# Row-group scores and a three-deep pipeline in linear attention; normalised probabilities, weighed two tiles at a time, in softmax attention

## The chip, the cores and the metric
The kernel runs on one core of a Trainium2 chip. The core's engines run side by side, each with its own queue, and wait for each other by semaphores: PE (TensorE, matmuls and transposes into PSUM), DVE (VectorE), ACT (ScalarE), POOL (GpSimd, SBUF only) and SP, which issues DMAs. The metric is the time of one execution on the device in microseconds; smaller is better.

## The reference
The input x is 2 sequences of 1024 tokens of 256 features. Two halves follow each other, all in fp32:

```
x = x + layernorm(linear_attention(layernorm(x)))          # 16 heads of 16, chunks
x = x + layernorm(h + moe(rmsnorm(h))),  h = t + attention(rmsnorm(t)),  t = layernorm(x)
```

The linear attention makes q = (x Wq f1 + b1)(x Wq f2 + b2), the same for k, and o = q (sum of earlier k'v) + masked(q k') v, then an rms norm over each head's 16 features and a projection. The kernel takes chunks of 128 tokens, which gives the same sums. The softmax attention is causal, with 32 query heads of 64 features and 8 key/value heads: scores, softmax, weighing of the values, projection. Then every token goes to its best 2 of 8 experts.

## The kernel before
Each engine has its own program; the order of work is written out by hand. A semaphore counts steps, and a later step waits for a count.

**Linear attention.** A step `s` of 8 handles 128 tokens of both batch entries (a pair of tiles). `pair_step(s, front, back)` exists on each engine: its front makes xn (normalised x), its transpose xnT, four feature products (q1, q2, k1, k2), qT and kT, v, the scores and kv of tiles `s`; its back makes output, rms norm, projection, residual and the norms of tiles `s-1`, and writes them turned into `rT_all`. So each step runs the front of one pair and the back of the one before; steps 1 to 7 are a hardware loop. Scores (L1113 to L1121): `qx` holds q eight times, each time with all but one head's 16 rows set to zero by `headmask` (POOL for k=0, L457; ACT for k=1, L582); a matmul over all 128 rows then gives four heads' scores for 512 columns. DVE masks each of four halves of scores (L774). DVE also adds to the running state (L791) and adds the residual (L822). `power` (L443) on POOL is the inverse root, three times per back.

**Softmax attention.** There are 16 sequences (8 key/value heads times 2 batch entries), each of 8 query tiles `ct` of 128 tokens; tile number `t` runs over 128. A tile has 4 heads and ct+1 blocks of 128 keys, so its scores are 128 x 128(ct+1) for each head: 128 columns for the first tile, 1024 for the last. Step `t` of the main loop does, on PE in this order:

- `score(t,0)`, the values (`values`, L1313) of tile t-2, `score(t,1)`, a third of the blocks of tile t-1 turned (`turn_part`, L1301), `score(t,2)`, the second third, `project_out` of tile t-2 (L1322), `score(t,3)`, the last third, and `project` of an item of the next half sequence (L1253, or L1243 for v).

DVE takes the maximum of each head's scores and copies them to SBUF (`maximum`, L884), ACT makes the exponentials in place with their sums (`exponent`, L640). Scores have four PSUM banks for ct<4 and two double banks above. The turned blocks go through three banks in rotation (`bank_of`, order in `TURNS`), which the items share, and are copied to SBUF by ACT and DVE in turn (L648, L892; `evacuate_part`). The division by the row's sum comes last: DVE takes the reciprocals (L905), POOL spreads them over 64 columns (L500), PE turns those too (L1298, one more block per tile, `m == t % TB + 1`), and DVE multiplies the weighed values by them (L909) into `oT`. `acc` gets the projection added by DVE (L922).

The change touches these two parts and nothing behind them but semaphore counts.

Of the kernel before, what the change touches and what calls it, by code (L numbers as in the profile page):

```python
# [10 lines left out]
ALU = mybir.AluOpType  # L11
# [26 lines left out]
NCONST = 27  # L38
# [23 lines left out]
def blocks_before(t):  # L62

    n, ct = divmod(t, TB)
    return n * (PAIRS + TB) + ct * (ct + 1) // 2 + ct
# [9 lines left out]
TURNS = FIRST_ITEMS + [x for t in range(TILES + 1)  # L75
                       for x in ([(t - 1, m) for p in range(3) for m in third(t - 1, p)] if t else []) + ([item_of(t)] if t < TILES and item_of(t) else [])]
# [8 lines left out]
def build(nc, a, out):  # L85
    ctx = ExitStack()
    with ctx:
# [23 lines left out]

        def x_part(x, part):

            return x[:].rearrange("p (b t) -> p b t", b=BATCH)[:, :, 1:TB] if part else x[:].rearrange("p (b t) -> p b t", b=BATCH)[:, :, 0:1]
# [21 lines left out]
        headmask = sb("headmask", [P, HB])  # L136
        experts = sb("experts", [P, E])
# [32 lines left out]
        qx = part(at, n, "p (k b h c) -> p k b h c", k=KB, b=BATCH, h=HB)  # L170
        sm = part(at + n, n, "p (k b h c) -> p k b h c", k=KB, b=BATCH, h=HB)
# [29 lines left out]
        onT = pair_tile(6)  # L201
        st6 = sb("st6", [P, BATCH, 6])
        mv = sb("mv", [P, BATCH, 2])
        ve = sb("ve", [P, BATCH])
        rstd = sb("rstd", [P, BATCH])
# [19 lines left out]
        rbc = [part(2 * G * SEQ + 2 * TB * G * P + i * 2 * P, 2 * P, "p (j c) -> p j c", j=2) for i in range(2)]  # L225
        spread = [part(2 * G * SEQ + 2 * TB * G * P + (2 + i) * 2 * P, 2 * P, "p (j c) -> p j c", j=2) for i in range(2)]
# [3 lines left out]
        def turned_to(t, m):  # L230

            src = bank_of((t, m))
            if m == t % TB + 1:
                return rbc[t % 2], src[:, 0:2 * P].rearrange("p (j c) -> p j c", j=2)
            return pT[t % 2][m], src[:]

        def evacuated(j):

            return S("pT_odd" if j % 2 else "pT_even"), j // 2 + 1
        oT = sb("oT", [P, 2, P])  # L240
# [86 lines left out]
        def _(sp):  # L327
# [36 lines left out]
            sp.wait_ge(S("acc_done"), BATCH * NKV * TB - TB)  # L364
            sp.dma_start(h_v[:, 0:TB], acc[:, 0:TB]).then_inc(S("h_stored"), 16)
            sp.wait_ge(S("acc_done"), BATCH * NKV * TB)
# [29 lines left out]
        def _(gp):  # L396
# [39 lines left out]
            nc.gpsimd.memset(state[:], 0.0).then_inc(S("constants_ready"), 1)  # L436
            gp.wait_ge(S("constants_ready"), NCONST - 1)
            nc.gpsimd.tensor_scalar(bd[:], headmask[:].rearrange("p (h o) -> p h o", o=1).to_broadcast([P, HB, DK]), 1.0 / DK, None, ALU.mult).then_inc(S("constants_ready"), 1)
# [12 lines left out]
            def pair_step(s, front, back):  # L451
                if front:
                    gp.wait_ge(S("qT_ready"), s + 1)
                    if front and back:
                        gp.wait_ge(S("scores1"), 4 * s)
                    for b in range(BATCH):
                        nc.gpsimd.tensor_tensor(qx[:, 0, b], qT[:, 0, b:b + 1, :].to_broadcast([P, HB, P]),  # L457
                                                headmask[:].rearrange("p (h o) -> p h o", o=1).to_broadcast([P, HB, P]),
                                                ALU.mult).then_inc(S("qx0_ready"), 1)
                if back:  # L460
                    for name in ("ao", "x1", "y"):
                        power(s - 1, BATCH, rstd[:], ve[:], "ve_" + name, "rstd_" + name)

            pair_step(0, True, False)
            x_power(1)
            with gp.Fori(1, TB) as s:
                pair_step(s, True, True)
            pair_step(TB, False, True)

# [19 lines left out]
            doubled = 1  # L489
            for t in range(TILES + 1):  # L490
                item = item_of(t - 1) if t else None
                if item and item[1] == 0:
                    if t > 1:
                        gp.wait_ge(S("rinv_spread"), t - 1)
                    double(item[0], item[2])
                    doubled += 1
                if t:
                    gp.wait_ge(S("k_doubled"), doubled)
                    gp.wait_ge(S("rinv_ready"), t)
                    nc.gpsimd.tensor_copy(spread[(t - 1) % 2].rearrange("p x (u d) -> p x u d", u=2),  # L500
                                          rinv[:, (t - 1) % 2].rearrange("p (u x o) -> p x u o", x=2, o=1).to_broadcast([P, 2, 2, DH])).then_inc(S("rinv_spread"), 1)
# [31 lines left out]
        def _(act):  # L533
# [18 lines left out]
            def pair_step(s, front, back):  # L552
                if front:
                    act.wait_ge(S("xnT_psum"), s + 1)
                    if back:
                        act.wait_ge(S("v_psum"), s)
                    nc.scalar.copy(whole(xnT[:]), bank[3][:]).then_inc(S("xnT_ready"), 1)
                if back:
                    act.wait_ge(S("o_psum"), s)
                    if front:  # L560
                        act.wait_ge(S("oms_psum"), s - 1)
                    nc.scalar.activation(whole(osq), bank[2][:], ACT.Square).then_inc(S("osq_ready"), 1)
                if front:
                    act.wait_ge(S("q1_psum"), s + 1)
                    if back:
                        act.wait_ge(S("qT_ready"), s)
                    nc.scalar.activation(whole(q1s), bank[0][:], ACT.Identity, bias=fbias_q[:, 0:1], scale=DK ** -0.5).then_inc(S("q1_ready"), 1)
                if back:
                    act.wait_ge(S("oms_psum"), s)
                    if front:  # L570
                        act.wait_ge(S("orstd_ready"), s - 1)
                    nc.scalar.activation(oms[:], bank[3][:], ACT.Sqrt, bias=eps[:, 0:1]).then_inc(S("oms_ready"), 1)
                if front:
                    act.wait_ge(S("k1_psum"), s + 1)
                    if back:
                        act.wait_ge(S("kT_ready"), s)
                    nc.scalar.activation(whole(k1s), bank[0][:], ACT.Identity, bias=fbias[:, 2:3]).then_inc(S("k1_ready"), 1)
                    act.wait_ge(S("qT_ready"), s + 1)
                    if back:
                        act.wait_ge(S("scores1"), 4 * s)  # L580
                    for h in range(HB):
                        ins = nc.scalar.activation(qx[:, 1, :, h], qT[:, 1], ACT.Copy, scale=headmask[:, h:h + 1])  # L582
                    ins.then_inc(S("qx1_ready"), 1)
                    act.wait_ge(S("v_psum"), s + 1)
                    if back:
                        act.wait_ge(S("kv_psum"), s)
                    for b in range(BATCH):
# [4 lines left out]
                if back:  # L592
                    tile = x_pairs(acc, s - 1)
                    act.wait_ge(S("y_ready"), s)
                    if front:
                        act.wait_ge(S("yss_ready"), s - 1)
# [3 lines left out]
                    wait_alone(act, S("rstd_y"), s)  # L600
                    if front:
                        act.wait_ge(S("rT_psum"), s - 1)
                    for b in range(BATCH):
                        ins = nc.scalar.activation(rn[:, b], tile[:, b], ACT.Copy, scale=rstd[:, b:b + 1])
                    ins.then_inc(S("r_ready"), 1)
                    act.wait_ge(S("rT_psum"), s)
                    for k in range(KB):
# [826 lines left out]
```

## Time and profile before

| what | value |
|---|---|
| median of 3 runs | 1934.72 us (1933.41 to 1934.87) |
| the profiled execution's own time | 1933.22 us |
| its span, first to last instruction | 1931.3 us |
| busy share: PE, DVE, ACT, POOL | 94%, 55%, 48%, 14% |
| chain that ended last: PE, DVE, ACT | 86%, 7%, 2% |
| mean granted TensorE clock | 0.976 |

The span is what the trace covers; 1.9 us of the execution lie around it. The chain that ended last is followed back from the last instruction to what released it each time; PE's share in it says on whose work the end hung. PE's busy time counts an instruction until its results have landed, so that back-to-back instructions overlap, and a busy PE is not one at its peak; its true pace shows in the distance between starts.

### The profile page before, as it was taken

The numbers are of one execution on the slowest core, as the hardware profiler recorded it, in microseconds if no ns is written. First come the engines' busy times: TensorE is split into PE (matmuls) and PEld (weight loads), VectorE is DVE, ScalarE is ACT, GpSimd is POOL, SyncE is SP. The second block draws the span as 40 slices with busy tenths as digits, with TensorE's granted clock in tenths as the row PEclk, the third lists the DMA queues.
The fourth block names the chain that finished last, engine by engine and source line by source line (L and its number), as shares of the span: only waits on it lengthen the run. The fifth ranks groups of instructions, "written<-read, shape, count | busy, mean of one in ns | idle before, by whom it ended". The sixth has DMA issues, their size and how long they took to land.

```text
span 1931.3 us, 32217 instructions
## 1 busy us (share of the span) xinstructions
PE 1813.6 (94%) x12286; PEld 1428.7 (74%) x12286; DVE 1055.0 (55%) x2465; ACT 924.1 (48%) x2049; POOL 261.1 (14%) x355
## 2 busy tenths in 40 slices
PE   6999689999999999999999999999985999999994
PEld 5666457777777777777777777777765999999993
DVE  3666556766776766767767667667655111111112
ACT  3343255655656656656656656656651222222223
POOL 2222110000000000000000000000001222222222
PEclk9999889999999999999999999999986999999997
DMA  2000010000000000000000000000017134213443
GB/s 83 0 0 0 0 44 1 9 1 1 9 1 1 9 1 1 10 1 1 9 1 1 9 1 1 1 1 1 23 34 245 22 92 128 48 26 87 119 125 95
DMA packets 46042, 60.02 MB, mean 31 GB/s; under 512 B 8944, under 2 KB 39536, under 8 KB 45936
## 3 DMA queue, kind: packets, MB, share of 16 engines
q1 hardware_dynamic: 36336, 46.16, 7.2%
q0 software_dynamic: 7536, 10.36, 3.2%
q10 hardware_dynamic: 2064, 2.10, 0.3%
q8 instruction: 66, 1.08, 0.2%
q14 instruction: 40, 0.33, 0.1%
HBM read 138.43 MB, written 11.40 MB: 78 GB/s over the span
## 4 chain that ended last, share of the span: by engine, by line
PE 86%; DVE 7%; ACT 2%; issue 2%; POOL 1%; DMA 1%; SPq 0%; DVEq 0%; POOLq 0%; ACTq 0%
PE wide L1401 15%; PE bank L1313 13%; PE bank L1301 12%; PE bank L1253 9%; PE wide L1285 8%; PE bank L1410 7%; PE wide L1286 7%; PE bank L1322 6%; PE wide L1120 2%; PE bank L1109 2%; PE bank L1298 1%; ACT qhl L634 1%; PE bank L1177 1%; DVE arena L802 1%; PE bank L1243 1%
## 5 line engine op out<-in xcount | busy, mean ns | idle before, releaser
L884 DVE CUSTOM_DVE_ANT_0 arena<-wide,arena 128x896 f32<-128x896 f32 (+7 forms) x512 | 383.8, 755 | 223.2 <-PE wide L1286 219.3
L640 ACT ACTIVATE arena<-arena,nmax 128x896 f32<-128x896 f32 (+7 forms) x512 | 397.0, 776 | 177.3 <-DVE nmax L884 174.2
L1285 PE MATMUL wide<-khi,qhl 128*128 128x512 f32 (+3 forms) x768 | 346.3, 452 | 1.7 <-DVE qhl L877 1.7
L1301 PE MATMUL bank<-ident,arena 128*128 128x128 f32 x2304 | 308.5, 274 | 0.0
L648 ACT COPY arena<-bank 128x512 f32<-128x512 f32 (+1 forms) x352 | 191.7, 545 | 214.0 <-PE bank L1301 206.3
L1401 PEld LDWEIGHTS wide<-wo,arena 128*128 128x128 f32 x2496 | 287.0, 193 | 3.2 <-issue 1.3
L1401 PE MATMUL wide<-wo,arena 128*128 128x128 f32 x2496 | 287.3, 277 | 0.9 <-ACT wo L693 0.9
L1313 PE MATMUL bank<-arena,vt 128*64 128x256 f32 x2304 | 277.0, 385 | 0.0
L1301 PEld LDWEIGHTS bank<-ident,arena 128*128 128x128 f32 x2304 | 262.3, 141 | 16.6 <-issue 0.4
L1286 PE MATMUL wide<-klo,qhl 128*128 128x512 f32 (+3 forms) x768 | 256.0, 347 | 0.0
L1050 DVE TENSOR_TENSOR wo<-wide,wo 128x512 f32<-128x512 f32 x78 | 53.9, 692 | 368.1 <-PE wide L1401 368.1
L892 DVE COPY arena<-bank 128x512 f32<-128x512 f32 (+1 forms) x352 | 222.9, 639 | 9.2 <-PE bank L1301 8.4
L1313 PEld LDWEIGHTS bank<-arena,vt 128*64 128x64 f32 x2304 | 154.2, 137 | 90.8 <-issue 19.9
L1285 PEld LDWEIGHTS wide<-khi,qhl 128*128 128x128 f32 x768 | 145.3, 189 | 89.3 <-issue 65.6
L1286 PEld LDWEIGHTS wide<-klo,qhl 128*128 128x128 f32 x768 | 146.2, 190 | 36.9 <-issue 22.5
L500 POOL COPY arena<-rinv 128x256 f32<-128x256 f32 x128 | 51.0, 398 | 784.4 <-DVE rinv L905 782.4
L1322 PE MATMUL bank<-wo,oT 128*128 128x256 f32 x512 | 135.1, 387 | 11.3 <-DVE oT L909 11.3
L1410 PE MATMUL bank<-arena,wo 128*128 128x256 f32 x624 | 141.2, 380 | 0.0
L703 ACT ACTIVATE wo<-wide 128x512 f32<-128x512 f32 x78 | 46.6, 597 | 170.3 <-PE wide L1401 170.3
L1410 PEld LDWEIGHTS bank<-arena,wo 128*128 128x128 f32 x624 | 115.8, 191 | 13.9
L1253 PE MATMUL bank<-rT_all,wq_g 128*128 128x512 f32 x256 | 122.5, 602 | 0.3
L1322 PEld LDWEIGHTS bank<-wo,oT 128*128 128x128 f32 x512 | 87.3, 191 | 24.3 <-DVE oT L909 14.7
(221 smaller groups left out, 1749.8 us busy)
## 6 DMA issues: line engine op xcount, KB each, us to landing
arena<-in_L_ffn_w SPq DMA_DIRECT2D x117, 1024.0 KB
x_all<-in_L_attn_x ACTq DMA_DIRECT2D x1, 2048.0 KB, 9.9
wq_g<-in_L_ffn_wq SPq DMA_DIRECT2D x8, 256.0 KB, 3.5
wo<-in_L_ffn_wo SPq DMA_DIRECT2D x16, 128.0 KB, 3.0
hbuf<-acc SPq DMA_DIRECT2D x2, 1024.0 KB, 4.6
tbuf<-rT_all SPq DMA_DIRECT2D x4, 512.0 KB, 3.0
acc<-hbuf SPq DMA_DIRECT2D x4, 512.0 KB, 5.5
out<-x_all SPq DMA_DIRECT2D x8, 256.0 KB, 2.1
```

Of the source, the lines that this page charges most:

```text
L640: nc.scalar.activation(probs[t % 2][:, h, 0:w], probs[t % 2][:, h, 0:w], ACT.Exp, bias=nmax[:, t % 2, h:h + 1], scale=-1.0, accum_out=rsum ...
L648: nc.scalar.copy(*turned_to(t, m)).then_inc(S("pT_even"), 1)
L884: nc.vector.tensor_tensor_reduce(out=probs[t % 2][:, h, 0:w], in0=score_bank(t, h)[:, 0:w], in1=causal[:, SEQ - w:SEQ], scale=-1.0, scalar ...
L892: nc.vector.tensor_copy(*turned_to(t, m)).then_inc(S("pT_odd"), 1)
L1253: ins = mm(to, w, rT_all[:, k, at:at + HALF], start=(k == 0), stop=(k == KB - 1))
L1285: mm(dst, q, khi[:, lo:lo + cols], start=True, stop=False)
L1286: ins = mm(dst, q, klo[:, lo:lo + cols], start=False, stop=True)
L1301: ins = nc.tensor.transpose(to[:, h * P:(h + 1) * P], probs[t % 2][:, h, m * P:(m + 1) * P], ident[:])
L1313: ins = mm(bank[2][u * DH:(u + 1) * DH, 0:2 * P], vt[:, n % 2, m], pT[t % 2][m][:, u * 2 * P:(u + 1) * 2 * P], start=(m == 0), stop=(m == ct))
L1322: ins = mm(bank[2][:, 2 * P:2 * P + D], oT[:, j], wo2[:, t // (BATCH * TB), j], start=(j == 0), stop=(j == 1))
L1401: ins = mm(wide[:, at + half, f * P:(f + 1) * P], w[:, k, (half * 4 + f) * P:(half * 4 + f + 1) * P], sT[u][:, k], start=(k == 0), stop=(k ...
L1410: ins = mm(bank[u][:, 0:D], gated[:, f], w2_e[u][:, f], start=(f == 0), stop=(f == FB - 1))
```

## The change
In linear attention the scores use four groups of 32 rows. `qx` holds q only twice (`rowmask`, heads even or odd within a group's 32 rows), and each matmul takes 32 rows and 256 columns into its own bank. The pipeline gets a third stage (output in step s+1, norms in s+2, turning in s+3), the loop is written out, the state and the residual are added on POOL, ACT normalises x (`normal_x`) and copies the projection's output (`aos`) out of PSUM.

In softmax attention DVE multiplies the probabilities by the reciprocal (`normalise`) before PE turns them; the spread block is gone, ACT copies all turned blocks and `oT`. The values of tiles t-3 and t-2 are weighed in one run, in steps of even number, into one bank, their projections go into a bank of the rotation, and one addition takes both.

```diff
-NCONST = 27
+NCONST = 29
+ROWS = 4
+HR = HB // ROWS
 def third(t, p):
-    blocks = t % TB + 2
+    blocks = t % TB + 1
     return range(blocks * p // 3, blocks * (p + 1) // 3)
+def weighed_in(t):
+    return [x for x in (t - 3, t - 2) if 0 <= x < TILES] if t % 2 == 0 else []
+STEPS = TILES + 3
+def turns_of(t):
+    turning = 1 <= t <= TILES
+    blocks = [[(t - 1, m) for m in third(t - 1, p)] if turning else [] for p in range(3)]
+    out = [("O", t)] if weighed_in(t) else []
+    item = [item_of(t)] if t < TILES and item_of(t) else []
+    return blocks[0] + blocks[1] + out + blocks[2] + item
...
 # POOL, linear attention
+                if back:
+                    power(s - 2, BATCH, rstds["ao"], ves["ao"], "ve_ao", "rstd_ao")
+                    gp.wait_ge(S("aon_ready"), s - 1)
+                    xb = x_pairs(x_all, s - 2)
+                    nc.gpsimd.tensor_tensor(xb, xb, aon, ALU.add).then_inc(S("x1_ready"), 1)
+                if mid and s < TB:
+                    gp.wait_ge(S("o_psum"), s)
+                    gp.wait_ge(S("kvt_ready"), s)
+                    nc.gpsimd.tensor_tensor(state, state, kvt, ALU.add).then_inc(S("state_ready"), 1)
...
 # DVE, order of a linear attention step
+                mask(s-1, 2), mask(s-1, 3); variance(ao), aon; qT; variance(x1); two reciprocals; kT; onT; y; mask(s, 0), mask(s, 1); ve_y; kvt
...
 # ACT, softmax attention
             def evacuate_part(t, p):
                 for m in third(t, p):
                     j = blocks_before(t) + m
-                    if j % 2 == 0:
-                        act.wait_ge(S("pT_psum"), j + 1)
-                        nc.scalar.copy(*turned_to(t, m)).then_inc(S("pT_even"), 1)
+                    act.wait_ge(S("pT_psum"), j + 1)
+                    nc.scalar.copy(pT[t % 2][m], bank_of((t, m))).then_inc(S("pT_ready"), 1)
...
                 if scored:
                     exponent(t, 0)
+                if weighed_in(t):
+                    n = 2 * P * len(weighed_in(t))
+                    act.wait_ge(S("o2_psum"), t // 2)
+                    nc.scalar.copy(oT[:].rearrange("p x j c -> p (x j c)")[:, 0:n], bank[2][:, 0:n]).then_inc(S("oT_ready"), 1)
...
 # DVE, softmax attention
+            def normalise(t, h):
+                w = (t % TB + 1) * P
+                if h % 2 == 0:
+                    invert(t, h // 2)
+                    v.wait_ge(S("rinv_ready"), 2 * t + h // 2 + 1)
+                nc.vector.tensor_scalar(probs[t % 2][:, h, 0:w], probs[t % 2][:, h, 0:w], rinv[:, t % 2, h:h + 1], None, ALU.mult).then_inc(S("probs_ready"), 1)
...
                 if scored:
                     maximum(t, 0)
+                if turning:
+                    normalise(t - 1, 2)
+                    normalise(t - 1, 3)
                 if item:
                     low_part(item)
...
                 if scored:
                     maximum(t, 2)
+                    normalise(t, 0)
+                if weighed_in(t):
+                    (adds the projection of both tiles to acc)
                 if scored:
                     maximum(t, 3)
+                    normalise(t, 1)
...
 # PE, linear attention
+                def score(k):
+                    pe.wait_ge(S("qx0_ready" if k == 0 else "qx1_ready"), s + 1)
+                    if s or k:
+                        pe.wait_ge(S("sm_ready"), 4 * s + 2 * k)
+                    for b in range(BATCH):
+                        for j in range(ROWS):
+                            rows = slice(j * P // ROWS, (j + 1) * P // ROWS)
+                            ins = mm(wide[:, j, b * HR * P:(b + 1) * HR * P], kT[rows, k, b], qx[rows, k, b].rearrange("p h c -> p (h c)"), start=True, stop=True)
 # order: output(0), turn xn, turn rn, feature 0, output(1), feature 1, mean square, features 2 and 3, v, turn kT, score(0), ao, kv, score(1)
...
 # PE, softmax attention
                     if m == 0:
-                        pe.wait_ge(S("exp_done"), G * (t + 1))
+                        pe.wait_ge(S("probs_ready"), G * (t + 1))
...
-                if weighing:
-                    values(t - 2)
+                if weighed_in(t):
+                    values(t)
```

Lines that begin with ` #`, and those that name steps in words, stand for longer stretches of the diff.

## Rows read from the trace of the kernel before

**Rows 1.** The page, part 1: busy time, share of the span, instructions.
```profile
PE 1813.6 (94%) x12286; PEld 1428.7 (74%) x12286; DVE 1055.0 (55%) x2465; ACT 924.1 (48%) x2049; POOL 261.1 (14%) x355
```

**Rows 2.** Windows: length, busy per engine, PE clock, DMA share, GB/s.
```profile
40.50:220.50 180.00, 168.92 (x1275) 118.92 (x1274) 117.76 (x204) 70.72 (x166) 40.87 (x35) 1.00 0.00 0
220.50:245.80 25.30, 8.87 (x112) 6.07 (x111) 10.66 (x21) 4.81 (x13) 2.09 (x3) 0.69 0.00 1
254.70:1428.00 1173.30, 1156.95 (x7405) 853.48 (x7406) 815.05 (x1948) 713.74 (x1563) 88.69 (x190) 1.00 0.02 4
```

**Rows 3.** Timeline, linear attention: start, length, engine, line, operation [idle before it].
```profile
117.94 0.43 PE L1131 MATMUL bank<-wo,arena 128*32 128x128 f32 x8
...
121.57 2.00 PE L1109 MATMUL bank<-arena 128*128 128x256 f32 x8
...
125.18 1.75 DVE L795 RECIPROCAL arena<-arena 128x256 f32<-128x256 f32 x1 [2.78 <-ACT arena L572]
...
127.67 3.75 POOL L457 TENSOR_TENSOR arena<-wo,headmask 128x1024 f32<-128x1024 f32 x2 [12.08 <-DVE wo L799]
...
128.50 3.29 ACT L582 ACTIVATE arena<-wo,headmask 128x256 f32<-128x256 f32 x8
...
133.94 3.60 PE L1120 MATMUL wide<-arena,wo 128*128 128x512 f32 x8
...
137.36 1.23 DVE L774 TENSOR_TENSOR arena<-wide,tri 128x1024 f32<-128x1024 f32 x1
...
138.50 0.72 DVE L831 TENSOR_SCALAR acc<-x_all,mv,rstd  x2
...
138.64 1.98 PE L1120 MATMUL wide<-arena,wo 128*128 128x512 f32 x4 [1.10 <-DVE arena L774]
139.14 1.22 DVE L774 TENSOR_TENSOR arena<-wide,tri 128x1024 f32<-128x1024 f32 x1
...
143.60 0.43 PE L1131 MATMUL bank<-wo,arena 128*32 128x128 f32 x8
```

**Rows 4.** Timeline: score(t,1) of the first tile of two successive sequences.
```profile
690.53 0.33 PE L1285 MATMUL wide<-khi,qhl 128*128 128x128 f32 x1
...
763.98 0.33 PE L1285 MATMUL wide<-khi,qhl 128*128 128x128 f32 x1
```

**Rows 5.** Timeline around a run of weighing and the maximum behind it.
```profile
1190.51 0.40 PE L1286 MATMUL wide<-klo,qhl 128*128 128x512 f32 x1
...
1190.84 2.81 PE L1313 MATMUL bank<-arena,vt 128*64 128x256 f32 x24
...
1193.91 0.40 PE L1286 MATMUL wide<-klo,qhl 128*128 128x512 f32 x1
...
1194.38 0.40 PE L1286 MATMUL wide<-klo,qhl 128*128 128x512 f32 x1
...
1194.82 1.23 DVE L884 CUSTOM_DVE_ANT_0 arena<-wide,arena 128x1024 f32<-128x1024 f32 x1 [0.55 <-PE wide L1286]
...
1195.97 0.08 DVE L884 DVE_READ_ACCUMULATOR2_ANT nmax<- 128x1 f32 x1
```

**Rows 6.** Timeline, end of the linear attention.
```profile
245.80 3.78 PE L1253 MATMUL bank<-rT_all,wkv_g 128*128 128x512 f32 x4 [0.93 <-ACT rT_all L608]
```

**Rows 7.** Groups by shape, softmax attention: busy us, mean ns | idle before, releaser.
```profile
L892 DVE COPY arena<-bank 128x512 f32<-128x512 f32 x288 | 196.5, 687 | 8.5 <-PE bank L1301 8.4
L640 ACT ACTIVATE arena<-arena,nmax 128x1024 f32<-128x1024 f32 x64 | 73.7, 1151 | 15.7 <-DVE nmax L884 15.7
...
L1298 PE MATMUL bank<-ident,arena 128*128 128x128 f32 x256 | 48.9, 273 | 1.4 <-POOL arena L500 1.4
```

**Rows 8.** Groups by shape, linear attention's loop: the same columns.
```profile
L819 DVE TENSOR_SCALAR arena<-bank,mv,rstd 128x256 f32<-128x256 f32 x14 | 7.0, 539 | 5.7 <-POOL rstd L443 5.7
...
L831 DVE TENSOR_SCALAR acc<-x_all,mv,rstd x14 | 5.1, 406 | 0.0
```

**Rows 9.** Groups by shape, softmax attention: the reciprocal.
```profile
L905 DVE RECIPROCAL rinv<-rsum 128x4 f32<-128x4 f32 x128 | 22.0, 172 | 3.5 <-ACT arena L640 0.8
```

More of the change, by code:

```diff
@@ L488, in _ @@
             double(0, 0)
[L489 to L501, printed above, removed]
+            for n in range(NSEQ):
+                for half in range(2):
+                    if n or half:
+                        double(n, half)
             gp.wait_ge(S("k_doubled"), 2 * NSEQ)
@@ L616, in _ @@
             act.wait_ge(S("ln_loaded"), 16 * (2 * KB + 1))
-            pair_step(0, True, False)
-            with act.Fori(1, TB) as s:
-                pair_step(s, True, True)
-            pair_step(TB, False, True)
+            normal_x(0)
+            for s in range(TB + 3):
+                pair_step(s)
             def evacuate(item):
@@ L653, in _ @@
                 evacuate(item)
-            for t in range(TILES + 2):
+            for t in range(STEPS):
                 scored, turning = t < TILES, 1 <= t <= TILES
@@ L1170, in pair_step @@
                     feature(bank[1], 3, "k2_psum")
-                if back:
+                    if mid:
+                        pe.wait_ge(S("oms_ready"), s)
+                    for b in range(BATCH):
+                        for k in range(KB):
+                            ins = mm(bank[3][:, b * D:(b + 1) * D], xnT[:, k, b], wvT[:, k], start=(k == 0), stop=(k == KB - 1))
+                    ins.then_inc(S("v_psum"), 1)
+                    pe.wait_ge(S("kT_ready"), s + 1)
+                    turn(bank[1], lambda k, b: kT[:, k, b], "ktok_psum")
+                    score(0)
+                if mid:
                     pe.wait_ge(S("onT_ready"), s)
@@ L1200, in pair_step @@
                     ins.then_inc(S("kv_psum"), 1)
[L1201 to L1211 removed]
+                    score(1)
+            for s in range(TB + 3):
+                pair_step(s, s < TB, 1 <= s <= TB, s >= 3)
             pe.wait_ge(S("rT_ready"), TB)
@@ L1326, in _ @@
                 project(item)
-            for t in range(TILES + 2):
-                scored, turning, weighing = t < TILES, 1 <= t <= TILES, t >= 2
+            for t in range(STEPS):
+                scored, turning = t < TILES, 1 <= t <= TILES
                 if scored:
                     score(t, 0)
-                if weighing:
-                    values(t - 2)
+                if weighed_in(t):
+                    values(t)
                 if scored:
@@ L1340, in _ @@
                     turn_part(t - 1, 1)
[L1341 to L1342 removed]
+                if weighed_in(t):
+                    project_out(t)
                 if scored:
```

419 lines of the change are left out of this document (193 added, 226 removed).

## The prediction
> **What bounds the kernel now.** I read the page's busy shares first: PE is busy 94% of the span, no other engine over 55% [rows 1]. A busy PE says little here, so the windows come next, one per stage, to see where the kernel spends its time: the linear attention's loop 180 us, its tail 25 us with PE busy 8.9 us, the softmax attention 1173 us [rows 2]. The router and experts behind them are not touched. Then the timeline, for start-to-start times, which a group's mean duration does not give. One loop step of the linear attention takes 143.60 - 117.94 = 25.66 us. One of the 16 sequences of the softmax attention takes 763.98 - 690.53 = 73.45 us [rows 3, 4].
>
> What PE must do in them. Eight feature instructions of 256 columns take 2.00 us, the last of them some 0.38 in flight: 0.213 each, 1.71 a feature [rows 3]. So 128 columns cost 0.107 an instruction, and an fp32 matmul is two. Linear step: 4 features 6.8, scores 8 matmuls of 512 columns 6.8 (eight instructions of them in 3.60, 0.43 each [rows 3]), both projections 3.4, two outputs 2.6, three turns 1.3, kv 0.85, mean square 0.85: 22.6, and 3.1 of waiting, 1.1 of it at L1120 for a mask [rows 3]. Softmax attention: a block of 128 keys costs 0.427 each in scores, turning and weighing, and a sequence has 36: 46.1; output projections 8 x 0.85 = 6.8; the next sequence's projections 11.0; spreads 8 x 2 x 0.107 = 1.7: 65.6. A run of weighing costs more than its columns: from 1190.51 to 1193.91 are 3.40 us, less two score slots of 0.235 and 24 x 0.107 = 0.37 us around it [rows 5]; call it 0.4, eight times 3.2. That makes 68.8, and 4.6 us of 73.45 are waits. PE bounds both, with little to spare in the second.
>
> **Linear attention, part by part.** Scores go from 128-row matmuls on eight head-masked queries to four 32-row matmuls each on two, 16 matmuls of 256 columns: the same 6.8 us if they run one after the other, a quarter, 1.7, if four row groups run together. No row shows row groups. The nearest are the four 32-column groups of L1131 and L1133: eight instructions that would take 0.85 us end after 0.43 with their flight [rows 3], so groups do run side by side in fp32. I take 1.7 and 0.4 for each of the two runs of another shape: 2.5, ends 1.7 and 6.8. Of the Trainium skill, TensorE: Matmul & The Clock Gate, Part 3 (Packing small matmuls), gives 3.07 times for four row groups with K=32 and 512 columns; by an estimate from it the scores are 2.2 us. TensorEngine Tiling (Array Packing), Key Properties, says that a change of tiling mode drains the engine, which agrees with the 0.37 us around a run.
>
> PE then has 22.6 - 6.8 + 2.5 = 18.3 us a step. DVE decides the rest. From the start of output(0): two masks until 2.5 (1.15 apart, as L774 to L831 [rows 3]); the projection's statistics, POOL's power and the shift until 5.4; idle until features 0 and 1 and output(1) are through (7.7), qT 8.5; statistics of x1 9.8; two reciprocals of 1.7 [rows 3] 13.2; kT 13.9. PE turns kT (14.4) and scores k=0 (15.6), two masks end at 18.0, and score(1) closes the step at 19.3 to 19.5. The moved state and residual additions (some 1 us each on POOL, estimated from DVE's 0.7 us for such tiles) lie beside this; POOL loses masking work of 3.8 us and ACT 2.5 of 3.3. The extra copy of the projection's output and the shift of x on ACT (0.6 and 0.8) lie beside feature work; ACT has some 11 us in 19. Seven steps save 7 x 6.2 = 43. The lighter first step saves 1. The start saves 2: one less mask behind the first kv, less the wait for ACT's first shift. The last tile now leaves through two partly filled steps: output, mean square, reciprocals, projection, then statistics, three powers, turn, 27 us from the last full step against 25.2 before, from 220.5 [rows 2] to the projection at 245.80 [rows 6]. Sum **-45 us**; with serial row groups a step is 4.5 longer, -13.
>
> **Softmax attention, part by part.** Gone: the spreads' 1.7 us of PE a sequence [rows 7], four of eight weighing runs' surroundings, 1.6, and PE's waits for the product L909. DVE loses all copies of turned blocks (288 of 512 columns, 196.5 us [rows 7]) and gains four normalisations a tile. ACT, which had 288, gets all 576, and a 512-column copy per pair of tiles. PE's necessary work is 65.6 - 1.7 + 1.6 = 65.5.
>
> Price of a normalisation. Same operation, same shape, 256 columns: 539 ns from PSUM, 406 ns from SBUF, 133 ns less, just what 128 columns cost at the maximum's 1.04 ns each [rows 8]; two follow each other in 138.50 to 139.14, 0.32 each [rows 3]. So I take 0.19 + 0.52 us per 1000 columns: 0.26 for 128, 0.73 for 1024. The other end, 1.04 per 1000 as DVE's maximum takes (1.15 for 1024, from 1194.82 to 1195.97 [rows 5]), is 1.26.
>
> What is late next. Until now a step had one tile's weighing between score(t,0) and score(t,1), which hid the way from the last exponential to the first turn. Now odd steps have none. There the first turn needs the last normalisation of the tile before, and that stands on DVE behind maximum(t,0), which waits for score(t,0). Path from the step's start, for 1024 columns: score 0.85; 0.2 until DVE starts (1194.38 + 0.235 against 1194.82); maximum 1.15; reciprocal with its wait 0.2 (0.18 itself [rows 9]); two normalisations of 896 columns 1.32; end and hand-over 0.18: 3.9. PE has two scores, 1.7: it waits 2.2 us. The same for 768, 512, 256 columns gives 1.9, 1.6 and 0.8 (there four scores and no block precede). Together **6.5 us** a sequence.
>
> ACT comes on top in the step of 1024 columns: four exponentials of 1.14 (1151 ns and a read, overlapping [rows 7]), seven copies of 0.48 to 0.6, two query copies 1.1: 9.5 us, and it idles for score and turn some 2.9. PE's blocks use three banks in rotation, so block 5 waits for copy 2, which stands behind the second exponential, and the item behind the last turn waits for copy 4, behind the third. Laid out step by step that is 1.9 more. By the same laying out the step of 768 columns gets 0.2 more, the first turn at 640 columns waits 0.5 (exponential 3 of the step before is late), and the even step that turns eight blocks 0.5 at its output projection. The other even steps wait for nothing: 9 blocks of weighing cover DVE and ACT.
>
> Steps 0 to 7: PE work 13.2, 3.0, 9.8, 3.4, 9.8, 6.4, 13.2, 6.8, waits 0.5, 0.8, 0, 1.6, 0.5, 2.1, 0, 4.1 (rounded; both sums before rounding are 65.5 and 9.6). A sequence takes **75.1 us**, 1.65 more than before, 16 times +26. So the pairing costs what the spreads and the saved runs bring, and a little more. Ends: 72.4 (only the first turns wait) and 78.2 (normalisation at one column a cycle).
>
> **Sum.** Span 1931.3, own time 1933.2; -45 + 26 = 1914.4; the median of the runs is 1.5 above the profiled execution: **1916 us**.
>
> **Rivals.**
> A. ACT keeps up: copies of turned blocks fit between exponentials and only the first turns wait. For it: ACT is busy 714 of 1173 us now [rows 2], and even steps give slack. Against: the slack is on the wrong side of the odd steps. 72.4 x 16 is 17 less than before: 1934.7 - 45 - 17 = 1873.
> B. The first turns don't wait either, since PE falls behind DVE anyway. Then only the removed 3.3 a sequence counts, -53: 1837. Against: maximum(t,0) can't start before PE's own score.
> C. The other side: normalisation runs at one column a cycle. Each of the 32 of a sequence costs up to 0.53 more, and two are on each odd step's path: 2 x 0.52 x 2.05 = 2.1 us, and DVE's eight-block step grows past ACT's, some 1.0. 3.1 x 16 = +50: 1966. It decides from about 0.91 us for 1024 columns on, where the whole change is even. For it: it reads and writes one tile in place, which no row shows. Against it are the two prices, with and without PSUM [rows 8]. VectorE: DVE Perf Modes, The perf-mode tier table, of the Trainium skill, says that fp32 tensor_scalar in SBUF runs at twice the rate, against C.
> D. Row groups run one after the other: the linear part gives 13 instead of 45: 1948. For it: no row shows them. Against: column groups do overlap.
>
> **How the numbers follow.** Forecast 0.50, A 0.19, B 0.07, C 0.11, D 0.10, other 0.03. The forecast's own range is 1895 to 1938, for waits of 8 to 11 us a sequence and a linear step of 19 to 20. For 8 in 10 it reaches towards A and D: 1864 to 1950. A measurement here tells 0.2%, about 4 us. Faster: forecast 0.45, A, B: 0.71. Slower: forecast 0.03, C, D and other: 0.24. Same 0.05.
>
> **What would show it.** Right: 16 sequences of 75 us; PE's wait before the first turn near 2 us in every second step, released by DVE's normalisation, and none in the others; normalisations of 1024 columns near 0.8 us; at 1024 columns PE also waits for ACT's copies; linear steps of 19.5 us with score groups under 1.5 us, and no L1120-like wait for masks beyond the last. Wrong: normalisations over 1.2 us (C), score groups of 3.4 us (D), no wait before first turns (B), waits there but ACT idle at the eight-block step (A).

## The result: 1941.8 us, slower by 7.6 us

| | median, us | runs from | to |
|---|---|---|---|
| before | 1934.23 | 1932.27 | 1935.16 |
| after | 1941.8 | 1940.78 | 1943.65 |

The ratio is 1.004, with a 95% interval of 1.0027 to 1.0053. The forecast was 1916 us and faster. The time lies inside the range for 8 in 10 (1864 to 1950), but outside the forecast's own range (1895 to 1938) and on the other side of no change. The profiled execution of after has a span of 1939.0 us and a time of its own of 1940.78.

The page of after, part 1, as [rows 1] of before:

```profile
PE 1740.0 (90%) x12158; PEld 1398.8 (72%) x12158; DVE 1031.4 (53%) x2547; ACT 1049.4 (54%) x2314; POOL 208.1 (11%) x236
```

PE has 74 us less to do, in a span that is 8 us longer: 81 us more of idle PE. The windows say where (as [rows 2]; the second and third row answer to the tail and to the softmax attention, the first holds seven steps of the linear loop):

```profile
41.40:178.40 137.00, 134.46 (x1382) 107.87 (x1378) 95.86 (x160) 59.24 (x135) 36.19 (x38) 1.00 0.01 1
178.40:206.30 27.90, 10.03 (x122) 6.80 (x118) 14.09 (x35) 8.42 (x24) 6.72 (x8) 0.70 0.00 1
214.70:1438.00 1223.30, 1120.66 (x7151) 835.14 (x7152) 811.57 (x2060) 847.02 (x1852) 37.82 (x62) 0.99 0.02 4
```

The linear loop runs almost without a gap now. In the softmax attention PE's busy time fell by 36 us, yet the stage grew by 49: PE idles 102.6 us in it, where before it idled 16.3 [rows 2]. The next rows are the timeline of after: the start, one full linear step, the end of the linear attention, and two successive sequences of the softmax attention.

```profile
21.60 1.28 ACT L651 ACT_TABLE_LOAD   x1
...
24.36 0.63 PE L1128 MATMUL bank<-ident,arena 128*128 128x128 f32 x4 [3.41 <-ACT arena L578]
...
25.67 8.86 PE L1134 MATMUL bank<-arena 128*128 128x256 f32 x32 [0.68 <-ACT arena L587]
...
41.41 0.42 PE L1157 MATMUL bank<-wo,arena 128*32 128x128 f32 x8
...
119.72 0.43 PE L1157 MATMUL bank<-wo,arena 128*32 128x128 f32 x8
...
122.50 1.99 PE L1134 MATMUL bank<-arena 128*128 128x256 f32 x8 [0.24 <-ACT arena L587]
...
134.34 1.15 PE L1146 MATMUL wide<-arena,wo 32*128 32x256 f32 x16
...
135.42 1.99 PE L1216 MATMUL bank<-arena,wo 128*128 128x256 f32 x8
135.56 2.36 DVE L819 TENSOR_TENSOR arena<-wide,tri 128x1024 f32<-128x1024 f32 x2 [0.62 <-PE wide L1146]
...
138.24 1.15 PE L1146 MATMUL wide<-arena,wo 32*128 32x256 f32 x16
...
139.31 0.43 PE L1157 MATMUL bank<-wo,arena 128*32 128x128 f32 x8
...
178.50 0.43 PE L1157 MATMUL bank<-wo,arena 128*32 128x128 f32 x8
...
206.32 3.78 PE L1273 MATMUL bank<-rT_all,wkv_g 128*128 128x512 f32 x4 [0.93 <-ACT rT_all L591]
...
356.11 0.33 PE L1305 MATMUL wide<-khi,qhl 128*128 128x128 f32 x1
...
356.27 0.27 PE L1306 MATMUL wide<-klo,qhl 128*128 128x128 f32 x1
...
356.47 5.83 PE L1330 MATMUL bank<-arena,vt 128*64 128x256 f32 x52
...
432.57 0.33 PE L1305 MATMUL wide<-khi,qhl 128*128 128x128 f32 x1
```

A linear step takes 139.31 - 119.72 = 19.59 us, and the projections behind the linear part start at 206.32, where it was 245.80 [rows 6]: 39.5 us earlier. A sequence takes 432.57 - 356.11 = 76.46 us, where it was 73.45 [rows 4]. The first score comes 40.0 us earlier (214.79 against 254.75), first score to last projection is 1223.3 us against 1173.9 before: +49.4, and behind it 1.8 us are won. The sum is -40.0 + 49.4 - 1.8 = +7.6, as the two spans differ (7.6 us).

**Where a sequence loses.** The step of eight column blocks without a weighing, in the timeline of after, from its scores to its first turn:

```profile
1111.13 0.79 PE L1305 MATMUL wide<-khi,qhl 128*128 128x512 f32 x1
1111.48 0.20 ACT L676 ACTIVATION_READ_ACCUMULATOR arena<-arena,nmax 128x1 f32 x1
...
1112.65 1.23 DVE L908 CUSTOM_DVE_ANT_0 arena<-wide,arena 128x1024 f32<-128x1024 f32 x1 [1.82 <-PE wide L1306]
...
1113.15 0.40 PE L1306 MATMUL wide<-klo,qhl 128*128 128x512 f32 x1
...
1113.80 0.16 DVE L921 RECIPROCAL rinv<-rsum 128x2 f32<-128x2 f32 x1
...
1114.00 1.28 DVE L916 TENSOR_SCALAR arena<-arena,rinv 128x896 f32<-128x896 f32 x2
...
1115.43 1.06 PE L1316 MATMUL bank<-ident,arena 128*128 128x128 f32 x8 [1.89 <-DVE arena L916]
```

The last exponential of the tile before is read out at 1111.48 + 0.20 = 1111.68. From there DVE could take its reciprocal and normalise. It sits idle until 1112.65, since the maximum of the new tile stands first in its queue and waits for PE's scores; reciprocal and normalisation come at 1113.80. PE has finished its two scores at 1113.55 and waits 1.89 us. Over the stage this is the group of waits that before did not have; the page's row of turns, and ACT's copies beside it:

```profile
L1316 PE MATMUL bank<-ident,arena 128*128 128x128 f32 x2304 | 317.3, 277 | 89.0 <-DVE arena L916 87.9
L683 ACT COPY arena<-bank 128x512 f32<-128x512 f32 x576 | 312.8, 588 | 141.8 <-PE bank L1316 141.2
```

Not all waits carry that name. The eight-block step ends on ACT's copies (timeline of after), which the prediction had as its second wait there. It is 0.96 us in 10 of 15 sequences and 0.1 us or less in the other five, 0.64 us as a mean over the 14 inner ones:

```profile
355.72 0.46 PE L1263 MATMUL bank<-ident,vT 64*128 64x64 f32 x4 [0.96 <-ACT arena L683]
```

The normalisation's price was the largest unknown. Its groups by shape, in the softmax attention of after:

```profile
L916 DVE TENSOR_SCALAR arena<-arena,rinv 128x1024 f32<-128x1024 f32 x64 | 46.7, 751 | 1.1
...
L916 DVE TENSOR_SCALAR arena<-arena,rinv 128x512 f32<-128x512 f32 x64 | 29.6, 485 | 1.1
...
L916 DVE TENSOR_SCALAR arena<-arena,rinv 128x128 f32<-128x128 f32 x64 | 20.8, 346 | 1.1
```

512 to 1024 columns add 266 ns, 0.52 per 1000, as predicted; 1024 columns take 0.75 us, not the 1.26 of rival C.

### The profile page after: what moved, and what is told of

It reads as the page before. It is cut to its first block, busy times and chain, and to the rows that moved or that the text cites. A ratio compares the mean times of both kernels' runs of the same rounds, so it can differ in the third digit from the quotient of the medians.

```text
span 1939.0 us, 31548 instructions
## 1 busy us (share of the span) xinstructions
PE 1740.0 (90%) x12158; PEld 1398.8 (72%) x12158; DVE 1031.4 (53%) x2547; ACT 1049.4 (54%) x2314; POOL 208.1 (11%) x236
## 4 chain that ended last, share of the span: by engine, by line
PE 82%; DVE 10%; ACT 5%; issue 1%; DMA 1%; POOL 1%; SPq 0%; POOLq 0%; DVEq 0%
PE wide L1421 14%; PE bank L1330 13%; PE bank L1316 11%; PE bank L1273 9%; PE bank L1430 7%; PE wide L1305 6%; PE bank L1342 6%; PE wide L1306 6%; DVE arena L908 3%; PE bank L1134 3%; DVE arena L916 3%; ACT arena L683 2%; ACT arena L676 2%; PE wide L1146 1%; PE bank L1216 1%
## 5 line engine op out<-in xcount | busy, mean ns | idle before, releaser
L1316 PE MATMUL bank<-ident,arena 128*128 128x128 f32 x2304 | 317.3, 277 | 89.0 <-DVE arena L916 87.9
L683 ACT COPY arena<-bank 128x512 f32<-128x512 f32 x576 | 312.8, 588 | 141.8 <-PE bank L1316 141.2
L1305 PE MATMUL wide<-khi,qhl 128*128 128x512 f32 (+3 forms) x768 | 330.4, 434 | 1.7 <-DVE qhl L901 1.7
L1330 PE MATMUL bank<-arena,vt 128*64 128x256 f32 x2304 | 263.0, 382 | 0.0
L916 DVE TENSOR_SCALAR arena<-arena,rinv 128x896 f32<-128x896 f32 (+7 forms) x512 | 258.2, 525 | 9.1
L1330 PEld LDWEIGHTS bank<-arena,vt 128*64 128x64 f32 x2304 | 159.6, 137 | 84.2 <-issue 7.9
L506 POOL CAST khi<-khi 64x512 fp32r<-64x512 f32 x32 | 19.5, 609 | 1071.8 <-ACT khi L666 1071.8
L1342 PE MATMUL bank<-wo,oT 128*128 128x256 f32 x512 | 123.0, 383 | 2.3 <-ACT oT L698 1.0
L698 ACT COPY oT<-bank 128x512 f32<-128x512 f32 (+1 forms) x65 | 37.4, 575 | 128.7 <-PE bank L1330 128.7
```

The costliest lines, as they stand in the source:

```text
L683: nc.scalar.copy(pT[t % 2][m], bank_of((t, m))).then_inc(S("pT_ready"), 1)
L916: nc.vector.tensor_scalar(probs[t % 2][:, h, 0:w], probs[t % 2][:, h, 0:w], rinv[:, t % 2, h:h + 1], None, ALU.mult).then_inc(S("probs_rea ...
L1305: mm(dst, q, khi[:, lo:lo + cols], start=True, stop=False)
L1316: ins = nc.tensor.transpose(to[:, h * P:(h + 1) * P], probs[t % 2][:, h, m * P:(m + 1) * P], ident[:])
L1330: ins = mm(bank[2][u * DH:(u + 1) * DH, x * 2 * P:(x + 1) * 2 * P], vt[:, n % 2, m], pT[t % 2][m][:, u * 2 * P:(u + 1) * 2 * P], start=(m ...
L1342: ins = mm(to[:, x * D:(x + 1) * D], oT[:, x, j], wo2[:, t // (BATCH * TB), j], start=(j == 0), stop=(j == 1))
```

## The experiments

The runs of each group share their runs of the kernel before: its median was 1932.7 us for the first four, 1932.9 for the next four and 1932.3 for the last two. Step times are start to start of each step's first score, taken from the traces, as a mean over the 14 inner sequences; steps 0 to 7 score 1 to 8 blocks of 128 keys:

```
step             0     1     2     3     4     5     6     7    sum
predicted     13.7   3.8   9.8   5.0  10.3   8.5  13.2  10.9   75.2
before        10.5   8.0   6.8   6.5   8.5   9.9  11.5  11.8   73.5
after         13.8   4.1  10.0   5.5  10.0   8.5  13.5  11.3   76.6
order         13.8   3.1  10.0   4.3  11.0   7.5  13.6  10.2   73.4
nonorm        13.8   3.1  10.0   4.3  10.0   7.4  13.5   9.8   72.0
odd_steps     10.7  12.0   5.1   7.9   7.3  11.8   9.9  14.5   79.3
single        10.3   7.9   6.9   6.5   8.3   9.7  11.0  11.5   72.1
single_order  10.3   7.9   6.5   6.1   8.3   9.6  11.0  11.5   71.2
```

**linear_only and attn_only: each part alone.** The kernel before with the diff's edits in the linear attention alone, or in the softmax attention alone.

> The linear attention as in the changed kernel, the softmax attention as before. If the two parts add up without touching each other, this gains the 40 us by which the softmax attention starts earlier in the changed kernel (214.7 against 254.7 us): 1894 us. If the gain is given back behind it (projections, clock), it is less, above 1900.

> The softmax attention as in the changed kernel, the linear attention as before. Additive theory: slower by 16 x (76.5 - 73.45) = 49 us, 1983 us, and a sequence of 76.5 us. If the changed linear part hands over a worse state (clock, timing), it is nearer to 1960.

Measured: linear_only 1892.58 us, ratio 0.9789 (0.9773 to 0.9806), 40 us less than before; attn_only 1981.35 us, ratio 1.0247 (1.023 to 1.0264), 49 us more. The two parts add up to what the whole change did (-40 + 49 = +9 against +7.6), so nothing that one part gave is lost to the other.

**single: the pairing undone.**

```diff
-    return [x for x in (t - 3, t - 2) if 0 <= x < TILES] if t % 2 == 0 else []
+    return [t - 2] if 0 <= t - 2 < TILES else []
```

(and the counts that go with it). Scaled probabilities and ACT's copies stay.

> The changed kernel with the pairing undone: each step weighs and projects one tile, t-2; normalised probabilities and ACT's copies stay. Theory 1 (the pairing empties the odd steps and lays the way exponential, maximum, normalisation, turn open): the waits before the first turn go, 7 us a sequence, ACT's lag in the eight-block step too, 2 us, and four runs of weighing come back, 1.6 us: 69 to 71 us a sequence, 1850 us (1835 to 1865). Theory 2 (scaled probabilities and copies by ACT alone are what is dear): a sequence stays at 75 us or more, 1918 us or more.

Measured: 1872.38 us, ratio 0.9689 (0.9672 to 0.9705). That is 69 us less than after: the pairing is the loss. Theory 2 is out: a sequence takes 72.1 us. Theory 1 had the direction, but had expected 22 us more, and the time lies outside its range. Against linear_only (1892.6) the scaled probabilities, the missing spread block and the copies on ACT together win 20 us. The page of single has the turns' wait for DVE gone, and what is left on ACT:

```profile
L1321 PE MATMUL bank<-ident,arena 128*128 128x128 f32 x2304 | 309.4, 274 | 2.4 <-DVE arena L921 1.2
...
L1278 PE MATMUL bank<-rT_all,wq_g 128*128 128x512 f32 x256 | 122.0, 599 | 10.8 <-ACT arena L688 10.8
```

**order: the pairs stay, DVE's queue changes.**

```diff
-                if scored:
-                    maximum(t, 0)
                 if turning:
                     normalise(t - 1, 2)
                     normalise(t - 1, 3)
+                if scored:
+                    maximum(t, 0)
```

> The changed kernel, pairs kept; DVE makes the last two normalisations of tile t-1 ahead of maximum(t,0) instead of behind it. Theory 1: the first turn of an odd step then hangs on exponential 3 and two normalisations only (1.9 us after the step's start at 1024 columns, where PE's two scores take 1.7), the waits there fall from 7 to about 2 us a sequence; maximum(t,0) is later by up to 1.5 us and with it ACT, so some returns as waits for copies: 72 to 74 us a sequence, 1880 us (1865 to 1905). Theory of ACT's load (copies by ACT alone set the odd steps): hardly any change, 1935 or more.

Measured: 1895.86 us, ratio 0.9811 (0.9794 to 0.9827), 46 us less than after, from two lines that swap places. The timeline of order, at the step shown above:

```profile
1001.29 0.79 PE L1305 MATMUL wide<-khi,qhl 128*128 128x512 f32 x1
...
1001.88 0.17 DVE L921 RECIPROCAL rinv<-rsum 128x2 f32<-128x2 f32 x1 [0.87 <-ACT arena L676]
...
1002.08 1.28 DVE L916 TENSOR_SCALAR arena<-arena,rinv 128x896 f32<-128x896 f32 x2
...
1003.28 1.22 DVE L908 CUSTOM_DVE_ANT_0 arena<-wide,arena 128x1024 f32<-128x1024 f32 x1
...
1003.55 1.04 PE L1316 MATMUL bank<-ident,arena 128*128 128x128 f32 x8
```

Scores to first turn are 2.26 us, where they were 4.30. The maximum comes a little later against its scores (1.99 us behind the step's start, it was 1.52), and step 4 pays 1 us for that; the other steps win 4.2.

**nonorm: no normalisation at all.** `normalise` loses its multiplication, and the turn waits for the exponential.

> The changed kernel with pairs, but the multiplication of the probabilities by the reciprocals left out (the output is not divided by the row sums), so that a turn waits for the exponential alone. In the changed kernel PE waits before first turns 7.8 us a sequence, in the trace for DVE's normalising. Theory 1 (those waits are DVE's queue: maximum of the next tile, then normalise, stand between the exponential and the turn): about 4.5 of the 7.8 us go, as in the run with the other order of DVE (3.3 us a sequence) and somewhat more since 258 us of DVE work go too: 72.2 us a sequence, 1880 us (1865 to 1895). Theory 2 (the exponential itself is late, ACT being behind with the copies of the weighed pair): the turns wait for ACT in place of DVE, and no more than 1 us a sequence goes: 1925 us or more.

Measured: 1869.65 us, ratio 0.9674 (0.9658 to 0.969), 72 us less than after, a little below theory 1's 1880. The run takes away two things at once, the place in DVE's queue and 258 us of DVE's work; it can't tell them apart. Its windows row for the softmax attention, with those of order, single and single_order behind it, each from its own trace:

```profile
214.30:1364.90 1150.60, 1121.96 (x7149) 828.91 (x7150) 575.02 (x1549) 844.94 (x1852) 37.80 (x62) 1.00 0.02 5
```

```profile
214.60:1392.20 1177.60, 1140.03 (x7151) 831.42 (x7152) 807.59 (x2060) 846.17 (x1852) 40.82 (x62) 1.00 0.02 5
```

```profile
213.00:1365.80 1152.80, 1135.49 (x7149) 825.11 (x7148) 819.07 (x2109) 863.54 (x1916) 37.75 (x62) 1.00 0.02 5
```

```profile
215.10:1355.40 1140.30, 1128.95 (x7151) 826.08 (x7151) 814.53 (x2109) 858.23 (x1915) 41.92 (x62) 1.00 0.02 5
```

Idle PE: nonorm 28.6 us, order 37.6, single 17.3, single_order 11.4, after 102.6. These are lower bounds, since a wait shorter than the flight of the last result isn't counted: order does the same PE work as after and shows 19 us more of busy PE, so the times decide. With the way through DVE cut away altogether, pairs still take 10 us more than single weighings that pay for it.

**odd_steps: pairs in the odd steps.**

```diff
-    return [x for x in (t - 3, t - 2) if 0 <= x < TILES] if t % 2 == 0 else []
+    return [x for x in (t - 3, t - 2) if 0 <= x < TILES] if t % 2 else []
```

(and the counts that go with it).

> The changed kernel, pairs weighed and projected in odd steps instead of even ones. Theory 1 (any step without a weighing leaves its first turn to wait for exponential and normalisation of the tile before, since nothing stands between scores and turns): the waits move to steps 0, 2, 4 and 6, about 3.0 + 0.9 + 1.6 + 1.9 = 7.4 us a sequence, no less than now: 1940 us (1925 to 1960). Theory 2 (the loss comes from the pairing falling on the wrong steps: the longest step without a weighing is the one of eight column blocks, which alone waits 2.8 us): with the weighing in the long odd steps about half of the 7.8 us goes: 1895 us (1880 to 1910).

Measured: 1989.34 us, ratio 1.0285 (1.0268 to 1.0303). Theory 2 is out; the direction is theory 1's, the size is beyond its range. The longest wait now lies in the bare step that scores a single block and turns eight: PE idles 2.67 us before its first turn. All idle PE of a sequence is 6.9 us by the trace, in after it is 6.3; most of the 2.7 us that a sequence takes longer is slower work (PE busy 1158.9 us against 1120.7). The timeline of odd_steps there:

```profile
917.43 1.42 DVE L921 TENSOR_SCALAR arena<-arena,rinv 128x1024 f32<-128x1024 f32 x2
...
919.00 1.94 PE L1321 MATMUL bank<-ident,arena 128*128 128x128 f32 x8 [2.67 <-DVE arena L921]
...
921.05 2.78 PE L1321 MATMUL bank<-ident,arena 128*128 128x128 f32 x12
```

Behind the wait the same eight turns take 1.94 us instead of 1.06, and twelve 2.78 instead of 1.5: PE works at the lower clock (the last section).

**single_order: both edits.**

> The kernel with the pairing undone (1872.4 us), and DVE normalises heads 2 and 3 of the tile before ahead of the new tile's first maximum. Theory 1 (with a weighing in each step the first turn has cover, its waits being 1.5 us a sequence in all, most of it 0.3 us behind a run of weighing that no DVE order can take away): no gain, 1872 us (1866 to 1877). Theory 2 (DVE's order is a loss in each step): 1 us a sequence goes, 1856 us. Against it: the later maximum delays the exponential and, behind it on ACT, the copies that the weighing waits for; then up to 1885 us.

Measured: 1859.83 us, ratio 0.9619 (0.9603 to 0.9635), between the theories: 12.6 us less than single, and steps 2 and 3 carry it (0.4 us each). Where the first turn has cover, DVE's order is worth a quarter of what it is worth where it has none (46 us).

**single_shared: half of the copies back on DVE.**

> The kernel with the pairing undone (1872.4 us), and the copies of turned blocks shared again, odd-numbered ones on DVE (0.64 us each by the row of before), even ones on ACT. Theory 1 (what is left of waits lies behind ACT: 1.0 us a sequence before the last block in the step of three column blocks, 0.8 us before output projections): about 1.2 us a sequence goes, 1853 us (1845 to 1866). Theory 2 (ACT's waits are only the tail of a chain that PE closes in time elsewhere, and DVE's queue of maxima and normalisations is the scarcer one): the copies stand behind maxima in DVE's queue and hold up blocks and exponentials, 1885 us (1876 to 1900).

Measured: 1903.29 us, ratio 0.9845 (0.9829 to 0.9862), 31 us more than single. Theory 2 has the direction, and the time is 3 us beyond its range: an added 196 us on DVE (0.686 us a copy, not 0.64), in the middle of its queue, costs more than ACT's relief brings. So the move of all copies to ACT, which the prediction had charged with waits, is a gain. It is also what the 20 us of single hang on: with the copies shared as before, the scaled probabilities take 11 us more than linear_only. The rows of single_shared: DVE's copies, and PE's waits for DVE before turns and projections:

```profile
L926 DVE COPY arena<-bank 128x512 f32<-128x512 f32 x288 | 196.3, 686 | 15.9 <-PE bank L1341 15.9
```

```profile
L1341 PE MATMUL bank<-ident,arena 128*128 128x128 f32 x2304 | 314.4, 275 | 15.3 <-DVE arena L933 11.7 <-DVE arena L926 2.4
...
L1298 PE MATMUL bank<-rT_all,wq_g 128*128 128x512 f32 x250 | 119.3, 599 | 8.8 <-DVE arena L926 8.7
```

**start and single_order_start: the first normalised x on DVE.** ACT's `normal_x(0)` goes; DVE does the subtraction and product right behind its first statistics.

> The changed kernel, the first normalised x of the linear attention made on DVE right behind its own statistics (17 us), not on ACT behind the table load and the copies of wide (23.13 us). In the changed kernel PE idles 3.41 us before the first turn (24.36) and then runs at half the granted clock, 32 features in 8.86 us against 7.17 later. Theory 1 (the wait is ACT's, and the clock falls because of the wait): the turn comes at about 21.0, the features take some 7.2, step 1 starts near 36.8 in place of 41.4: 3.4 to 5 us less, 1937.5 us. Theory 2 (the clock falls at the start whatever PE does): only the wait goes, at most 3.4 us, and half of it is given back since DVE's statistics of the other tiles come 0.8 us later: 1939.5 us. The rest of the kernel is the same.

> Pairing undone, DVE normalises heads 2 and 3 before the next tile's first maximum (1859.8 us), and the first normalised x on DVE. If the start is worth 3.4 to 5 us by itself, 1855.5 us (1853 to 1858); the parts lie in different stages and should add. If DVE's later statistics hold up the first steps, 1859 us.

Measured: start 1939.7 us, 2.1 less than after, with runs from 1938.19 to 1941.11 against 1940.78 to 1943.65 for after; the ratios to their own runs of before, 1.0035 and 1.004, overlap; single_order_start 1854.41 us, ratio 0.9596 (0.9583 to 0.9609), 5.4 less than single_order (their runs of before differ by 0.6). The timeline of start:

```profile
21.20 0.63 PE L1132 MATMUL bank<-ident,arena 128*128 128x128 f32 x4 [0.72 <-issue]
23.28 7.17 PE L1138 MATMUL bank<-arena 128*128 128x256 f32 x32 [1.46 <-ACT arena L587]
...
37.34 0.42 PE L1161 MATMUL bank<-wo,arena 128*32 128x128 f32 x8
```

The time is the one that theory 2 gave, but the trace shows theory 1's mechanism: step 1 starts at 37.34, 4.1 us earlier, and the features take 7.17 us at the full clock. The first score comes 4.1 us earlier too (210.71 against 214.79). Half of that is gone again by the end, 0.7 us of it up to the first score of the last tile and 1.3 behind it: the span is 2.1 shorter. The trace of start has seven stretches of half clock inside the softmax attention, after has five; at 0.3 us each (below) that makes 0.6 of the 2 us, and the rest stays open. Nor do I know how these few us would repeat: start has one profile. With single weighings the softmax attention has no such stretch behind its first 6 us, and the whole gain arrives (first score 3.8 us earlier, span 3.7 shorter than in single_order). single_order_start is the fastest version, 78 us below before.

## Why the prediction was wrong

- **Linear attention, -45: 5 us too much, and the step's time in part by luck.** A step takes 19.59 us, forecast 19.3 to 19.5. But the forecast had 18.3 us of work for PE and DVE closing the step. In the trace DVE's two masks are ready at 18.2 us (135.56 + 2.36 - 119.72), nearly as laid out (18.0), and PE comes to score(1) only at 18.5 (138.24 - 119.72): its own work fills 19.35 us, it idles 0.24, for ACT. DVE does not close the step. A group of scores, 16 instructions, takes 1.08 us (134.34 to 135.42), where one after the other they would take 16 x 0.213 = 3.4: rival D is out. The factor of 3.07 that the Trainium skill gives for four row groups (TensorE: Matmul & The Clock Gate, Part 3) agrees with that, here it is 3.15. The tail took 27.8 against 27. The larger part that is missing stands at the start: 3 us were credited, and step 1 starts 0.9 us later than before (41.4 against 40.5 [rows 2]). ACT makes the first xn behind a table load, PE waits 3.41 us, and then runs at half clock. start, with this x on DVE, gets 4.1 us back there.
- **Attention, the price of a normalisation: right** (0.75 against 0.73 for 1024 columns; for 128 columns 0.35 against 0.26). By the Trainium skill's double rate for it (VectorE: DVE Perf Modes, The perf-mode tier table), the trace agrees: 0.52 us per 1000 columns, half of the maximum's 1.04.
- **Attention, the new wait: right in place and cause, a little too long.** Before the first turns of steps 1, 3, 5 and 7 PE idles 0.75, 1.29, 1.58 and 1.88 us, predicted 0.8, 1.6, 1.9 and 2.2: 5.5 in place of 6.5 us (some 6.2 if the flight of the last score, up to 0.17 us each, is counted as waiting).
- **The step that failed is "That makes 68.8, and 4.6 us of 73.45 are waits", and with it "A sequence takes 75.1 us".** The 4.6 us were never measured as waits; they are what the prices of PE's work left over. The profile shows 16.3 us of idle PE over the 16 sequences of before [rows 2], 1.0 a sequence. The other 3.6 are work that the prices miss, and they stay when the waits change. The forecast let all 4.6 go and put 9.6 in their place (only rival B kept them). The table sets PE's time of each step, less the idle time that the trace shows in it, beside the forecast; means over the 14 inner sequences of after:

```
step              0    1     2     3     4     5     6     7     sum
work, predicted  13.2  3.0   9.8   3.4   9.8   6.4  13.2   6.8   65.5
work, after      13.7  3.3  10.0   4.2  10.0   6.9  13.5   8.7   70.3
waits, predicted  0.5  0.8   0     1.6   0.5   2.1   0     4.1    9.6
idle PE, after    0.1  0.8   0     1.3   0     1.6   0     2.6    6.3
```

- **Two terms were off, against each other.** Work was 4.8 us too low, waits 3.3 too high (about 1 us less of each if flights are counted as waiting), and 1.5 us a sequence came out as the difference. That 75.1 lies only 2% from 76.6 is luck. Part of the missing work can be named: one head's scores of 128 columns take 0.36 us with the changes of kind before and behind them (356.11 to 356.47), where the price is 0.107, and a slot of 512 columns takes the 0.235 us that the prediction itself used for runs of weighing, not 0.213. The rest is not split up here. 16 times 1.5 is 23 us (+49 in place of +26), more than the forecast gain of 19. With the 5 us of the linear part this turns the sign.
- **"So the pairing costs what the spreads and the saved runs bring, and a little more"** can be held against two runs. The forecast has 16 x 3.35 = 54 us for the pairing (5.0 us more of waits a sequence, 1.6 less of work) and -27 for the missing spreads. Measured are 69 (after against single) and -20 (single against linear_only). The pairing saves 0.9 us of PE's work a sequence, by PE's busy time (1135.5 for single, 1120.7 for after), and idle time goes from 17 to 103 us in all, 5.3 a sequence.
- **ACT's lag.** Predicted as 3.1 us a sequence, it is 0.8. It is seen at the end of step 7 (0.96, in the trace put down to L683), hardly in step 0 (0.1 for 0.5) and not in step 4 (0 for 0.5). In its waits the kernel is nearer to rival A than to the forecast; A's 1873 failed on the work, as the forecast did. (A's 72.4 us don't come out of its terms either: 65.5 + 6.5 are 72.0.)
- **Rival B** fell: the first turns wait. **Rival C** gave the right side for a reason that the rows refute.
- **The chances.** Faster at 0.71 took two uncertain terms of 45 and 26 as if their difference were known to within 20. An error of 1 us a sequence was well within what hand laying can do, and it is 16 us. The parts of "slower" add up to 0.27, not 0.24. And the working took DVE's order as given: "that stands on DVE behind maximum(t,0)" was written down, priced, and its weight seen, but much of what made it costly was one swap away.

## What to carry to other kernels

Work that covers a hand-over (here a run of weighing between scores and turns) is not free to move: doing two in one step saves PE 0.9 us a sequence and lays bare four hand-overs of 0.8 to 1.9 us. If such a step must be bare, order each helper engine's queue by when its inputs are ready: DVE's finished exponentials waited behind a maximum whose scores were not there yet, and the swap returned 46 us. It does not make the pairing good: with the better order in both, pairs still take 36 us more (order against single_order). Time that priced work does not explain is not yet waiting; the idle time in the profile tells (here 1.0 us a sequence, not 4.6). When a forecast is the difference of two large terms, multiply the error that one period may have by the number of periods before giving a chance on the sign.

## What the chip showed that I had not expected

After a wait of PE near 2 us the granted clock fell to half, the 1.2 GHz level, for 3.4 us. The timeline and the windows of after, the eight-block step in another sequence: the first turn with its wait, the turns and scores behind the wait, then the rest of the step; the last row is the same place in the step shown above, with the same wait (1.89 us) and no fall.

```profile
1268.41 1.91 PE L1316 MATMUL bank<-ident,arena 128*128 128x128 f32 x8 [1.88 <-DVE arena L916]
```

```profile
1268.40:1271.80 3.40, 3.39 (x12) 2.94 (x13) 2.50 (x4) 1.99 (x3) 0.00 (x0) 0.51 0.00 0
1271.80:1275.60 3.80, 3.69 (x29) 3.16 (x27) 3.52 (x7) 3.54 (x9) 0.00 (x0) 0.99 0.00 0
1114.80:1118.00 3.20, 2.57 (x19) 2.38 (x20) 3.12 (x6) 1.44 (x4) 0.00 (x0) 1.00 0.00 0
```

In after this happened in five of the 16 sequences and cost about 0.3 us each (76.8 against 76.5 us), since the wait for ACT at the end of that step shrinks from 0.96 to 0.1 us. In odd_steps, where the bare step waits 2.67 us, it happened behind that wait in all 15 sequences that have it, and the clock of the whole stage shows it:

```profile
214.70:1488.00 1273.30, 1158.86 (x7178) 864.53 (x7178) 813.87 (x2049) 851.60 (x1854) 37.79 (x62) 0.97 0.02 5
```

At the start of the kernel the clock fell in all eight kernels in which ACT makes the first x and PE waits for it (3.41 us in after), and in none of the four in which DVE does (before, attn_only, start, single_order_start). So a wait can cost more than its length: it slows the work behind it. What decides whether the clock falls after equal waits no run here tells apart.
